# A mixture-of-experts stage whose W_i weights stay in SBUF, with the wait for landed accumulates on GpSimd

## The reference, cut to what matters

```
x = x + conv(groupnorm(x))                 # 16 images, 16x16 positions, 192 channels, float32
t = t + attn(layernorm(t))                 # gated attention over 256 positions of an image
t = t + ffn(layernorm(t))                  # 4096 tokens, 8 experts, top 2
# ffn:
router_logits = xf @ Wr.T
topk_vals, topk_idx = top_k(router_logits, 2); w = softmax(topk_vals)
h  = gelu(einsum('th,efh->etf', xf, Wi) + bi)        # 192 -> 768
eo = einsum('etf,ehf->eth', h, Wo) + bo              # 768 -> 192
out[t] = sum over the token's two experts of w * eo
```

## Time and profile before

| | |
|---|---|
| median of 3 runs | 713.14 us (712.94, 713.14, 720.59) |
| profiled execution, its own time | 708.21 us |
| its span | 706.5 us |
| convolution and attention stages | to about 316 us |
| third stage, pairs and singles | about 334 to 703 us |
| PE busy over the span | 612.7 us (87%) |
| DVE, ACT, POOL busy | 426.8, 363.8, 247.0 us |
| in the chain that ended last: the DMA to `out_rows` | 25% of the span |

### The profile page before, as it was taken

The page is one execution under the profiler, slowest core; times in us unless marked ns, Lnnn a source line. Parts: engine busy times, 40 slices in busy tenths (PEclk is TensorE's granted clock), DMA queues, the critical chain, the costliest instruction groups (busy, mean ns, idle before and its releaser), DMA issues.

```text
span 706.5 us, 14741 instructions
## 1 busy us (share of the span) xinstructions
PE 612.7 (87%) x3998; PEld 563.8 (80%) x3999; DVE 426.8 (60%) x1575; ACT 363.8 (51%) x779; POOL 247.0 (35%) x238
## 2 busy tenths in 40 slices
PE   4899996999999999982889888888898888889893
PEld 3898895888888888872788888787888788888893
DVE  4778886588888888886744334444334444344560
ACT  2323336677777786832655444455444454444551
POOL 3423221023444435353333334343233332334232
PEclk9899998899999999996899999999999999999998
DMA  8700000001110101114474555444555445554641
GB/s 315 298 0 0 0 19 1 12 22 59 40 62 34 67 34 54 47 51 149 127 190 124 134 134 130 110 102 127 134 134 122 97 118 132 128 115 117 139 114 17
DMA packets 35958, 67.22 MB, mean 95 GB/s; under 512 B 4983, under 2 KB 27800, under 8 KB 35802
## 3 DMA queue, kind: packets, MB, share of 16 engines
q1 hardware_dynamic: 22328, 53.01, 24.0%
q0 software_dynamic: 13488, 13.74, 11.2%
q10 hardware_dynamic: 114, 0.15, 0.1%
HBM read 49.31 MB, written 17.57 MB: 95 GB/s over the span
## 4 chain that ended last, share of the span: by engine, by line
DMA 27%; issue 10%; PE 6%; POOL 5%; DVE 2%; POOLq 1%; DVEq 0%; SPq 0%
DMA out_rows<-const,y_id 25%; PE ps L1130 6%; POOL out_rows L638 4%; DVE const L1114 2%; DMA lists<-row_b,slots 1%; DMA lists<-pad_rows 1%; DMA conv_only<-lists 1%; POOL lists L613 0%; DVE y_id L1111 0%; POOLq L201 0%; POOLq L453 0%; PE ps L1134 0%; DVEq L1111 0%; POOLq L642 0%; PE ps L1135 0%
## 5 line engine op out<-in xcount | busy, mean ns | idle before, releaser
L638 POOL DMA_INDIRECT out_rows<-const,y_id x71 | 121.2, 1707 | 230.1 <-DVE const L1114 204.4
L762 ACT ACTIVATE hT<-ps,b_i_sb 128x256 f32<-128x256 f32 (+1 forms) x240 | 94.9, 447 | 150.9 <-PE ps L1130 150.9
L1130 PE MATMUL ps<-w_o_sb,hT 128*128 x852 | 151.1, 334 | 13.3 <-issue 12.2
L1130 PEld LDWEIGHTS ps<-w_o_sb,hT 128*128 128x128 f32 x852 | 140.4, 193 | 20.7 <-issue 20.7
L1107 DVE TENSOR_TENSOR const<-ps,b_o_sb 128x384 f32<-128x384 f32 (+1 forms) x40 | 20.5, 513 | 95.9 <-PE ps L1130 95.9
L1130 PE MATMUL ps<-sA_hi,we_hi 128*128 128x256 f32 (+1 forms) x240 | 72.4, 302 | 2.9 <-DVE sB L1092 1.8
L1084 DVE TENSOR_TENSOR we_lo<-we_in,we_hi 128x768 fp32r<-128x768 f32 x80 | 72.9, 952 | 0.2 <-ACT we_hi L752 0.2
L1130 PE MATMUL ps<-sA_lo,we_hi 128*128 128x256 f32 (+1 forms) x240 | 67.5, 281 | 0.0
L1130 PE MATMUL ps<-sB,we_hi 128*128 128x256 f32 (+1 forms) x240 | 67.4, 281 | 0.0
L1130 PE MATMUL ps<-sB,we_lo 128*128 128x256 f32 (+1 forms) x240 | 67.3, 281 | 0.0
L1130 PE MATMUL ps<-sA_hi,we_lo 128*128 128x256 f32 (+1 forms) x240 | 67.3, 281 | 0.0
(11 more groups left out here) (220 smaller groups left out, 1369.7 us busy)
## 6 DMA issues: line engine op xcount, KB each, us to landing
we_in<-in_w_i SPq DMA_DIRECT2D x40, 768.0 KB, 5.3
conv_only<-lists SPq DMA_DIRECT2D x31, 194.0 KB, 5.1
w_o_sb<-in_w_o SPq DMA_DIRECT2D x8, 576.0 KB, 11.4
out_rows<-X SPq DMA_DIRECT2D x16, 192.0 KB, 1.9
X<-in_x SPq DMA_DIRECT2D x1, 1536.0 KB, 13.0
out_rows<-const,y_id POOLq DMA_INDIRECT x71, 5.1
conv_only<-lists SPq DMA_DIRECT2D x9, 97.0 KB, 4.4
we_in<-in_w_hid SPq DMA_DIRECT2D x1, 768.0 KB, 8.3
```

The lines of the kernel that those rows point to most:

```text
L638: pool.indirect_dma_start(out=out, out_offset=bass.IndirectOffsetOnAxis(ap=y_id[:, odd, t:t + 1], axis=0), in_=y_sb[:, odd, t, :], in_offs ...
L762: last = act.activation(hT[:, odd, f, 0:n].unsqueeze(1), ps_h[:, b, c, 0:n].unsqueeze(1), ACT.Gelu, bias=b_i_sb[:, ds(e * FCHUNKS + f, 1)])
L1130: return pe.matmul(dst, lhsT, rhs, start=start, stop=stop)
```

## The change

All eight W_i are held in SBUF (`we_all`); six are loaded with the other parameters at the start, two (whose place serves the attention weights first) after `bias_done`. SP's `load_weights` is gone, and with it its `value_load`; ACT and DVE read the expert's number themselves and split W_i straight from `we_all`. To make room, `hT` also serves as `v_sb`, `gateT`, `gatedT` and `simT` of the attention stage, and `sA_hi`, `sA_lo`, `sB` become `nA_hi`, `nA_lo`, `nB`. DVE copies the ids to a new tile `y_row` and scales the rows without waiting for `added` of the tile before; it only waits, ahead of L1107's counterpart, for the accumulates of the tile two before, whose buffer it overwrites. GpSimd waits for `added`, then writes `y_id = y_row + 0`, waits for its own write, and issues the accumulates. PE reads the expert's number in the middle of `h`, ahead of chunk 3. The first tiles are written out instead of looped on GpSimd, and two more steps of DVE are written out ahead of its loop (`skip=2`).

```diff
@@ -160,7 +160,7 @@
         self.wait()
 
 
-def pipeline(eng, step, first, last, ahead, behind, unroll=1, parity=False, chain=None, per=0, upto=None):
+def pipeline(eng, step, first, last, ahead, behind, unroll=1, parity=False, chain=None, per=0, upto=None, skip=0):
 
 
 
@@ -171,7 +171,7 @@
         step(i, odd) if parity else step(i)
 
     n = last + 1 - behind
-    lo, hi = behind + 1, (n if upto is None else upto) - ahead
+    lo, hi = behind + 1 + skip, (n if upto is None else upto) - ahead
     hi -= (hi - lo) % unroll
     for i in range(first, lo):
         run(i, i % 2)
@@ -262,11 +262,15 @@
         nB_bias = sb("nB_bias", [KBB, SEQ], f32r)
 
         zT, qT, kT = (xc[0:QK, :, :, :].rearrange("p a t c -> p (a t c)")[:, n * SEQ:(n + 1) * SEQ] for n in range(3))
-        v_sb = sb("v_sb", [P, HALVES, HID])
-        gateT = sb("gateT", [P, HID // P, SEQ])
-        simT = sb("simT", [P, HALVES, SEQ])
+        hT = sb("hT", [P, 2, FCHUNKS, TWO])
+        in_hT = hT[:, :, :, :].rearrange("p b f n -> p (b f n)")
+
+        v_sb = in_hT[:, 0:HALVES * HID].rearrange("p (t c) -> p t c", c=HID)
+        gateT, gatedT = (in_hT[:, at * HID // P * SEQ:(at + 1) * HID // P * SEQ].rearrange("p (k n) -> p k n", n=SEQ)
+                         for at in (1, 2))
+        simT = in_hT[:, 3 * HID // P * SEQ:3 * HID // P * SEQ + HALVES * SEQ].rearrange("p (t n) -> p t n", n=SEQ)
+        assert HALVES * HID <= HID // P * SEQ
         attnT = sb("attnT", [P, HALVES, SEQ])
-        gatedT = sb("gatedT", [P, HID // P, SEQ])
 
 
         u_var = sb("u_var", [P, HALVES])
@@ -319,24 +323,22 @@
 
         w_hi = sb("w_hi", [P, 2, SLICE], f32r)
         w_lo = sb("w_lo", [P, 2, SLICE], f32r)
-        we_in = sb("we_in", [P, 2, 2 * FF])
+        we_all = sb("we_all", [P, EXPERTS, 2 * FF])
         we_hi = sb("we_hi", [P, 2, 2 * FF], f32r)
         we_lo = sb("we_lo", [P, 2, 2 * FF], f32r)
-        hid_in = we_in[:, 0, :].rearrange("p (k f) -> p k f", k=2)
-        b_hid_sb, b_hid_hi = (we_in[0:KBB, 1, n * SLICE:(n + 1) * SLICE] for n in range(2))
+        hid_in = we_all[:, EXPERTS - 1, :].rearrange("p (k f) -> p k f", k=2)
+        b_hid_sb, b_hid_hi = (we_all[0:KBB, EXPERTS - 2, n * SLICE:(n + 1) * SLICE] for n in range(2))
         b_i_sb = sb("b_i_sb", [P, EXPERTS * FCHUNKS])
         b_o_sb = sb("b_o_sb", [P, EXPERTS, D])
         slot_rows = conv_only[:, 0:4 * slot_width].rearrange("p (b t c) -> p b t c", b=2, t=2)
         meta = sb("meta", [P, MOE_TILES, 2, 2], i32)
-        sA_hi = sb("sA_hi", [P, TWO], f32r)
-        sA_lo = sb("sA_lo", [P, TWO], f32r)
-        sB = sb("sB", [P, TWO], f32r)
-        hT = sb("hT", [P, 2, FCHUNKS, TWO])
-
+        sA_hi, sA_lo, sB = nA_hi, nA_lo, nB
         y_at = CONST_AT["fwd0"][0]
         assert y_at + 4 * D <= CONST_AT["inv1c"][1]
         y_sb = const[:, y_at:y_at + 4 * D].rearrange("p (b t c) -> p b t c", b=2, t=2)
+        y_row = sb("y_row", [P, 2, 2], i32)
         y_id = sb("y_id", [P, 2, 2], i32)
+        no_offset = sb("no_offset", [P, 2], i32)
 
         ps = ctx.enter_context(nc.psum_tensor("ps", [P, 8, 512], f32))
 
@@ -367,7 +369,7 @@
         ld_const, ld_rest, ld_w1, ld_attn, ld_exp = (sem(f"ld_{n}") for n in ("const", "rest", "w1", "attn", "exp"))
         ld_x = [sem(f"ld_x{n}") for n in range(len(X_GROUPS))]
         ld_hid = sem("ld_hid")
-        we_in_done = [sem(f"we_in_{n}") for n in ("even", "odd")]
+        ld_wi, id_done = sem("ld_wi"), [sem(f"id_done_{n}") for n in ("even", "odd")]
         we_hi_done, we_done = sem("we_hi_done"), sem("we_done")
         hi_done, parts_done = sem("hi_done"), sem("parts_done")
         qk_hi_done, qk_parts_done = sem("qk_hi_done"), sem("qk_parts_done")
@@ -483,6 +485,8 @@
             sp.dma_start(b_o_sb[:, :, :], b_o.partition_broadcast(P)).then_inc(ld_attn, 16)
 
 
+            for e in range(EXPERTS - 2):
+                sp.dma_start(we_all[:, e, :], w_i[:, e, :]).then_inc(ld_wi, 16)
             for e in range(EXPERTS):
                 sp.dma_start(w_o_sb[:, e, :, :], w_o[:, e, :, :]).then_inc(ld_exp, 16)
 
@@ -499,12 +503,11 @@
                 sp.dma_start(ov[:, tiles(i), :], X[:, tiles(i), :]).then_inc(stored, 16)
 
 
+            sp.wait_ge(bias_done, 1)
+            for e in range(EXPERTS - 2, EXPERTS):
+                sp.dma_start(we_all[:, e, :], w_i[:, e, :]).then_inc(ld_wi, 16)
             with sp.Fori(0, IMAGES) as i:
                 store(i)
-
-            def load_weights(j, odd):
-                e = sp.value_load(tile_expert[0:1, ds(j, 1)], min_val=0, max_val=EXPERTS - 1)
-                sp.dma_start(we_in[:, odd, :].unsqueeze(1), w_i[:, ds(e, 1), :]).then_inc(we_in_done[odd], 16)
 
             def load_tile(j, odd):
                 at = sp.value_load(tile_row[0:1, ds(j, 1)], min_val=0, max_val=SPARE)
@@ -516,13 +519,10 @@
             sp.wait_ge(tiles_done, 2)
             sp.wait_ge(scattered, 16 * 2 * HALVES * (IMAGES - 2))
             for j in range(2):
-                load_weights(j, j)
                 load_tile(j, j)
             pad_lists(sp, range(EXPERTS // 2), padded)
 
             def load_next(j, odd):
-                wait_alone(sp, we_done, j - 1, ld_const)
-                load_weights(j, odd)
                 wait_alone(sp, sT_ps, j - 1, ld_const)
                 sp.wait_ge(meta_done, j - 1)
                 load_tile(j, odd)
@@ -556,6 +556,7 @@
             def set_up_lists():
 
                 chain.link(pool.memset(pad_rows[:, :], 0.0))
+                chain.link(pool.memset(no_offset[:, :], 0))
                 pool.wait_ge(ld_rest, 16)
                 chain.link(pool.tensor_copy(pad_rows[:, ID:ID + 1].bitcast(i32), K("pad_id")))
                 pool.tensor_copy(list_at[:, :], K("list_base")).then_inc(pads_ready, 1)
@@ -633,15 +634,22 @@
 
             def add_rows(j, odd, nth):
 
-                wait_alone(pool, y_done[odd], nth, ld_const)
-                for t in range(rows_of(j)):
+                n = rows_of(j)
+                pool.wait_ge(y_done[odd], nth)
+                wait(pool, added, added_before(j))
+                pool.tensor_tensor(y_id[:, odd, 0:n], y_row[:, odd, 0:n], no_offset[:, 0:n],
+                                   ALU.add).then_inc(id_done[odd], 1)
+                wait_alone(pool, id_done[odd], nth, ld_const)
+                for t in range(n):
                     pool.indirect_dma_start(
                         out=out, out_offset=bass.IndirectOffsetOnAxis(ap=y_id[:, odd, t:t + 1], axis=0),
                         in_=y_sb[:, odd, t, :], in_offset=None, compute_op=ALU.add).then_inc(added, 16)
 
-            with pool.Fori(1, PAIRS // 2 + 1) as nth:
+            for j in range(2):
+                add_rows(j, j, 1)
+            with pool.Fori(2, PAIRS // 2 + 1) as nth:
                 for odd in range(2):
-                    add_rows(0, odd, nth)
+                    add_rows((nth - 1) * 2 + odd, odd, nth)
             for j in range(PAIRS - 1, MOE_TILES):
                 add_rows(j, j % 2, j // 2 + 1)
 
@@ -742,18 +750,22 @@
 
             pipeline(act, attn_step, **ATTN)
 
+            act.wait_ge(ld_wi, 16 * EXPERTS)
+            act.wait_ge(tiles_done, 2)
+
             def moe_step(j, odd):
                 if not absent(j + 1, MOE_TILES):
 
-                    act.wait_ge(we_in_done[1 - odd], (j + odd) * 8 + 16)
+                    if isinstance(j, int) and j + 1 == FIRST_TILES:
+                        act.wait_ge(tiles_done, 6)
+                    e = act.value_load(tile_expert[0:1, ds(j + 1, 1)], min_val=0, max_val=EXPERTS - 1)
                     wait(act, h_ps, j * (FCHUNKS // 2))
                     for k in range(2):
                         here = slice(k * FF, (k + 1) * FF)
-                        act.activation(we_hi[:, 1 - odd, here], we_in[:, 1 - odd, here], ACT.Copy).then_inc(we_hi_done, 1)
+                        act.activation(we_hi[:, 1 - odd, here].unsqueeze(1), we_all[:, ds(e, 1), here],
+                                       ACT.Copy).then_inc(we_hi_done, 1)
                 if not absent(j, MOE_TILES):
                     n = rows_of(j) * P
-                    if isinstance(j, int) and j == FIRST_TILES:
-                        act.wait_ge(tiles_done, 6)
                     e = act.value_load(tile_expert[0:1, ds(j, 1)], min_val=0, max_val=EXPERTS - 1)
                     for b in range(FCHUNKS // 2):
                         act.wait_ge(h_ps, j * (FCHUNKS // 2) + b + 1)
@@ -1078,11 +1090,12 @@
                     dve.wait_ge(rows_in[1 - odd], (j + odd) * 8 + 16)
                     dve.tensor_copy(slot_rows[:, 1 - odd, 0:n, ROW:], slot_rows[:, 1 - odd, 0:n, DATA + KA:ROW]
                                     ).then_inc(twin_done, 1)
+                    e = dve.value_load(tile_expert[0:1, ds(j + 1, 1)], min_val=0, max_val=EXPERTS - 1)
                     for k in range(2):
                         here = slice(k * FF, (k + 1) * FF)
                         wait_alone(dve, we_hi_done, 2 * j + 3 + k, ld_const)
```

(22 more changed lines are left out.)

## The result

The changed kernel takes **659.7 us** (median of 4 runs, 658.64 to 661.38) against 715.14 (4 runs, 712.94 to 720.59): a ratio of 0.922, 95% interval 0.919 to 0.925. The forecast was 655 us, 645 to 680. The profiled execution took 660.72 us, its span is 658.7.

What follows compares the result with a forecast made beforehand. The ring of accumulates was taken to bound the pairs, with PE next at 7.95 us. Terms of start, intervals and singles summed to -58.1 us, 650.1 for the profiled 708.2; scaled by 0.7% to the median, 655 us, range 645 to 680.

Steps and rivals of the forecast that it cites:

- The ring of accumulates: Pairs, kernel before: landing, DVE's ids and scaling, GpSimd's two DMAs, landing again; 9.90 us, said to hold up PE.
- my 29 intervals: Third stage, `y` of tile 1 to that of tile 30: 278.2 us become 29 x 7.95 = 230.6, -47.6 us.
- The landing: Accumulates among the pairs: median 5.7 us falls to 4.2 once the W_i load beside them is gone; ends 3.6 and 5.7.
- What is left of the ring: Pairs, changed kernel, on GpSimd alone: 3.37 us plus landing, 7.6 us (7.0 to 9.1), under PE's 7.95.
- PE's and DVE's register loads, ACT: Third stage: added register loads cost nothing; PE's in mid-`h` bounded by 0.6 us in 40 tiles, 24 us.
- The early loads: First two stages: eight W_i loads of 768 KB cost nothing; at most the two late ones would show, 10.6 us.
- The start, -4.3: Start of the third stage: without W_i loads, scatters land sooner and PE's waits go, -4.3 us; bounds 1 and 8.
- Rival A: Pairs: GpSimd's ring still bounds, 9.1 us at a 5.7 us landing; 688 us, at half that 671; chance 0.19.
- Its second way: Pairs: GpSimd's id instruction held until one `we_lo` instruction of 0.91 us ends; ring 8.5 us, 16 us more, 671 us.
- B: Rival: PE's register load is exposed in mid-`h`, 0.6 us in 40 tiles, 24 us; 679 us; chance 0.05.
- C: Rival, pairs: accumulates' own traffic makes the landing long, ring stays 9.7 us, no gain there; 707 us; chance 0.05.
- D: Rival, pairs: slower, GpSimd's ring at a 7.0 us landing takes 10.4 us a pair; 728 us; chance 0.05.

Runs made afterwards that it cites:

- before, load held back: Kernel before, with SP holding each tile's W_i load from tile 5 on until the accumulates then under way have landed: 657.17 us, ratio 0.930.
- changed, with the unread load: Changed kernel plus a 768 KB W_i load for each tile from tile 2 on, into a buffer that nobody reads: 658.12 us, ratio 0.918.

## Why the prediction was right, and where it was off

- **What bounds the kernel, and what is next:** right. The ring of accumulates went, PE became the bound, at 7.93 us a pair for the 7.95 of the forecast. One of my 29 intervals, tile 29 to 30, already holds a single's `h` and took 7.45 us; that is 0.5 of the 1.1 us by which the term was too small. PE's own pace is 7.87 us in the two runs that still load W_i for use, and 7.94 in all with W_i in SBUF; why wasn't asked.
- **The landing, 3.7 us for 4.2:** right in size, and for a reason that doesn't hold in full. The medians of the second accumulates say more than those of both (load ahead of the second accumulate, its landing):

| kernel, 400 to 560 us | load ahead by | landing |
|---|---|---|
| before | -0.02 to 0.92 us, 0.04 in the median | 5.9 |
| wait on GpSimd alone | 0.57 to 1.87 | 4.5 |
| changed, with the unread load | 0.57 to 1.78 | 4.5 |
| before, load held back | 2.73 to 4.12 | 3.5 |
| changed | no load | 3.5 |

  The forecast's reason, that the landing needs the load *gone*, is the step that failed. It had no effect on this number, which was right by luck as far as the reason goes, but the two expectations built on it missed (9.1 us a pair, measured 7.86 and 7.91). The row of the singles that I took for "one accumulate alone" says so by itself. There the W_i load goes out 3.6 us ahead of the accumulate, is in the air for some 5 us, and the accumulate lands in 3.7:

```profile
658.41 0.34 SPq L507 DMA_DIRECT2D we_in<-in_w_i  x1
```

```profile
662.05 1.64 POOL L638 DMA_INDIRECT out_rows<-const,y_id  x1 [3.88 <-DVE const L1114]
```

  In the two runs with 4.5 us the meeting moved to the pair's first accumulate. The load is issued 0 to 1.3 us behind that one, which lands in 5.8 and 5.3 us in the median, but it has 1.9 us of head start on the second and doesn't close the ring. In the kernel before, the load goes out 1.9 to 2.2 us behind twelve of the 16 first accumulates, 0.2 us or more after GpSimd's instruction is over, and these land in 3.6 to 3.9 us. For the other four GpSimd takes 1.9 to 2.5 us, the load goes out before it is through, and they land in 6.7 to 7.0.

  The load's moment isn't the whole of it either: 0.9 us ahead gives 5.1 to 5.5 us in the kernel before, 0.6 ahead 4.5 with the wait on GpSimd. The rows' load follows 0.3 us behind the accumulate there and 1.8 here; that was not taken apart.
- **The ring:** the 5.7 us of the forecast is the median over both accumulates of a pair. The second alone has 5.9, and with the 3.76 us of the rest that gives the 9.7 us that a pair took. What is left of the ring in the changed kernel, waking taken from the run with the wait on GpSimd, is about 0.1 + 0.2 + 0.8 + 2.5 + 3.5 = 7.1 us (an estimate, since nothing waits for it), for the 7.6 of the forecast.
- **The two halves:** each gives the whole gain (ratios 0.924 and 0.921, the change 0.922), because both break the same meeting: one removes the load, the other moves the accumulates away from it. They don't add, since PE's own period, 7.9 us, lies under both.
- **PE's and DVE's register loads, ACT:** nothing, as said; for PE's the run without the move shows it. (The parts of one load in the earlier trace rows are 0.30 and 0.15 us; the 0.6 us of the forecast holds for the whole with the gaps between, not as 0.30 + 0.15 + 0.15.)
- **The early loads:** no cost in a trace with the short attention stage: that run's residual sums span 181.9 us against 182.0 before.
- **The start, -4.3:** -3.9 between the two traces, -5.1 against the second trace of the kernel before (44.7 us from the last residual sum to `y` of tile 1, for 39.7). The check that I gave for it, `y` of tile 1 later than 357 us, would have called it wrong: 368.12. An absolute time was a poor check, since all that comes before it, the 11 us of the attention stage too, is in it.
- **Rival A** was the right one to fear. Its second way, an id instruction held by `we_lo`, is real: 0.91 us in the run with the wait alone, where it ends 0.07 us behind `we_lo`, and 0.99 in the run with the unread load. In the changed kernel all 20 between 400 and 560 us take 0.19, because the landing there is over before DVE is through with the scaling, and the instruction runs ahead of `we_lo`. The Trainium skill, page SBUF — State Buffer, section Who interferes with whom, says that the later of two such instructions is blocked for the length of the first; the 0.91 us agrees. The forecast's 671 us for this case did not come: the meeting costs nothing as long as the ring stays under PE's period. **B** is refuted by the register load put back, **C and D** by the landing. Of the signs, the DMA share was off as well: 0.34 for 0.52, where I had said halved.
- **655 against 659.7:** I scaled the profiled execution by the 0.7% to the median. What lay between them was the attention stage: the trace of before had its short pattern (182.0 us), while the changed kernel's trace had the long one (193.1). That is a matter of 11 us in one stage, and of which chip and execution is traced, and not a common factor. On the chip with the short pattern the medians differ by 58.4 us (707.37 and 649.01), near the sum of the forecast. That 659.7 lies close to 655 owes something to luck: which patterns the two traces and the runs fell into was not forecast.

## What to carry to other kernels

When a DMA's landing closes a ring, look in the trace for what is issued within a microsecond of it, and move that first: one wait on SP gave here 50 of the 58 us that a rebuilt buffer plan gave. Look at each DMA by itself, not at a median over two kinds. Two remedies for the same meeting don't add, and once the next bound lies close under the ring, either is enough. Before explaining a difference, compare the parts of both traces that the change doesn't touch; what differs there may not be the change's.

## What the runs showed of the hardware

- **A direct load and an indirect accumulate issued together hurt the accumulate.** 768 KB issued at the moment of a 96 KB accumulate: landing 5.9 us in the median; 2.7 us or more ahead of it: 3.5, at a higher DMA share (0.64 for 0.52). Issued up to 1.3 us behind one, while GpSimd's instruction still runs, it lengthens that landing too (5.8 and 5.3 us). The share of busy DMA engines doesn't tell of such a meeting.
- **GpSimd's own time on an indirect DMA can grow beside DVE.** With `we_lo` over, or nearly, before they start, the 41 of the run with the wait on GpSimd take 1.55 to 1.58 us; beside it 2.18 (446.27 us) and 2.54. But nine in the run with W_i from SBUF alone run beside it for nearly their whole length and take 1.56, so running side by side isn't enough.
- **One program, two attention stages.** 12.1 us an image, or about 13.6 and 12.6 in turn, for the kernel before and the changed one alike. All four traces of the second chip are short; all six of the first and third are long, with three to five late releases each. PE has the same work in both, 179.4 and 179.3 us in 182.0 and 193.1 us. The residual sum of every second image then waits 1.2 to 1.5 us for something that the trace calls remote, when the matmuls that it reads have long been issued. What that is wasn't found. The chip alone may not decide it: runs of the kernel before on the first chip spread from 710.4 to 720.9 us, and only profiled ones show their pattern.
